# A two-layer attention and routed feed-forward block on one core: one VectorE subtraction a slot earlier, one group of weighted sums a step later

## The reference

```python
x = x + xattn(layernorm(x), ctx, ctx, w_q, w_k, w_v, w_o)      # 16 heads of 16, causal, softmax(q k / 4) v
q, k, v = (fff(layernorm(x), tree) for tree in "qkv")          # 4 routing levels, 16 leaves of 256 -> 64 -> 256
x = x + softmax(q k / 16) v
```

## Time and profile before

| What | Value |
|---|---|
| Median of 3 runs | 640.76 us (640.52 to 642.57) |
| Profiled execution, its own time | 640.1 us |
| Its span | 638.3 us |
| Mean granted TensorE clock | 0.965 |
| TensorE matmul busy | 586.1 us, 92% |
| VectorE busy | 439.1 us, 69% |
| ScalarE busy | 299.0 us, 47% |
| SyncE's DMA queue (q1) | 70.5% of 16 engines' time |

### The profile page before, as it was taken

One profiled execution on the slowest core, in us unless ns is written; L12 is line 12 of the kernel. 1 busy time (PEld: TensorE's weight loads), 2 busy tenths in 40 slices (PEclk: granted clock), 3 DMA queues, 4 the chain that ended last, 5 costly groups with the idle time before them and its releaser, 6 DMA issues.

```text
span 638.3 us, 14744 instructions
## 1 busy us (share of the span) xinstructions
PE 586.1 (92%) x5131; PEld 494.5 (77%) x5131; DVE 439.1 (69%) x1511; ACT 299.0 (47%) x482; POOL 236.9 (37%) x298
## 2 busy tenths in 40 slices
PE   8677999999899999999999897859999999799996
PEld 7566888877788887888888686848888888689995
DVE  2765666988788898898898787873555555156664
ACT  4104544544444453554445355007877787533331
POOL 6700010143143243334323326660006666666551
PEclk9869999999899999999999899879999999999999
DMA  6798788898998898899898749977999999766653
GB/s 190 221 305 261 237 230 226 252 260 238 283 271 249 286 310 247 258 297 283 251 296 275 208 134 303 309 254 274 324 364 387 411 408 375 258 191 197 200 177 126
DMA packets 99639, 169.58 MB, mean 266 GB/s; under 512 B 12848, under 2 KB 67824, under 8 KB 99568
## 3 DMA queue, kind: packets, MB, share of 16 engines
q1 hardware_dynamic: 87712, 141.83, 70.5%
q0 software_dynamic: 9216, 25.18, 12.5%
q10 hardware_dynamic: 2640, 1.65, 0.9%
HBM read 92.59 MB, written 75.50 MB: 263 GB/s over the span
## 4 chain that ended last, share of the span: by engine, by line
PE 51%; DMA 26%; SPq 13%; DVE 5%; issue 3%; ACT 1%; POOL 1%; DVEq 0%; ACTq 0%; POOLq 0%
DMA parts_dram<-k_lo 9%; DMA k<-parts_dram 8%; PE banks L840 6%; PE banks L825 6%; PE banks L814 6%; DMA parts_dram<-q_lo 5%; SPq L334 5%; PE banks L882 4%; PE banks L903 4%; PE banks L530 4%; PE banks L545 4%; PE banks L557 3%; SPq L317 2%; PE banks L871 2%; PE banks L573 2%
## 5 line engine op out<-in xcount | busy, mean ns | idle before, releaser
L1537 POOL DMA_INDIRECT xs_dram<-xn2s,place x96 | 95.7, 997 | 159.4 <-ACT pt L936 142.4
L1174 DVE TENSOR_REDUCE mneg<-banks 128x2 f32<-128x512 f32 x240 | 121.8, 548 | 44.9 <-PE banks L546 43.8
L936 ACT ACTIVATE pt<-banks 128x768 f32<-128x768 f32 x128 | 103.5, 810 | 102.2 <-PE banks L558 101.7
L545 PE MATMUL banks<-k,q 107*128 107x256 f32 x240 | 76.4, 369 | 17.7 <-DMA k<-parts_dram 10.9
L557 PE MATMUL banks<-q,k 109*128 109x256 f32 x256 | 74.0, 341 | 2.0 <-DMA q<-m_lo 0.3
L545 PEld LDWEIGHTS banks<-k,q 107*128 107x128 f32 x240 | 46.5, 194 | 29.3 <-DMA k<-parts_dram 16.3
L558 PE MATMUL banks<-q,k 109*128 109x128 f32 x256 | 57.3, 224 | 0.0
L573 PE MATMUL banks<-pt,vp 128*32 128x256 f32 (+1 forms) x1024 | 56.4, 339 | 0.4 <-ACT pt L936 0.4
L1596 POOL DMA_INDIRECT q_all<-ys_dram,place x32 | 30.8, 964 | 67.1 <-DMA ys_dram<-yb 53.8
L546 PE MATMUL banks<-k,q 107*128 107x128 f32 x240 | 54.4, 227 | 0.0
L557 PEld LDWEIGHTS banks<-q,k 109*128 109x128 f32 x256 | 48.7, 190 | 6.8 <-ACT pt L936 5.7
(11 more groups left out here) (177 smaller groups left out, 1290.9 us busy)
## 6 DMA issues: line engine op xcount, KB each, us to landing
ys_dram<-yb SPq DMA_DIRECT2D x36, 512.0 KB, 6.2
xb<-xs_dram SPq DMA_DIRECT2D x35, 512.0 KB, 7.7
k<-parts_dram SPq DMA_DIRECT2D x128, 128.0 KB, 3.8
q<-parts_dram SPq DMA_DIRECT2D x64, 256.0 KB, 4.6
xs_dram<-zero SPq DMA_DIRECT2D x45, 256.0 KB
xs_dram<-zero SPq DMA_DIRECT2D x18, 384.0 KB, 4.8
tables<-leafw SPq DMA_DIRECT2D x16, 257.0 KB, 8.2
xt<-x SPq DMA_DIRECT2D x16, 256.0 KB, 4.9
```

The source lines that it names most:

```text
L545: mm(ps[:, 0:S], q[0:KN, t, P:S], k[0:KN, t, :], start=True, stop=True)
L936: nc.scalar.activation(pt[:, 2 * p:2 * p + 2, :], st_banks(b, p)[:, :, 0:S + P], ACT.Exp, scale=SC).then_inc(exp_sb, 1)
L1174: last = nc.vector.tensor_reduce(mneg[1 - u][:, t, 2 * j:2 * j + 2], S_BANKS[:, :, cols], axis=AX.X, op=ALU.max, negate=True)
L1537: gp.indirect_dma_start(xs_dram[tree], bass.IndirectOffsetOnAxis(ap=place[:, k:k + 1], axis=0), xn2s[m % RING][:, t, :], None).then_inc(sc ...
```

## The change

On VectorE the subtraction for the low part of k of batch b + 2 moves from slot 4 (behind the maxima of that slot, ahead of `divide`) to slot 3, behind norm_in and ahead of part 4 of `allocate`. On TensorE, group 0 of the weighted sums of batches 0 to 14 moves from step b, slot 7, to step b + 1, slot 0, where it stands behind the transposes of the maxima and ahead of group 1. Group 1 thereby stands behind these transposes too; in step 15 it did before. The last batch keeps its group 0 at j = 6. No matmul, no transfer and no semaphore is added or removed.

```diff
-                    if j == 3 + lag(b) and has(b, 0):
+                    if j == 3 + lag(b) and b == NB - 1:
                         weigh(b, u, 0)
                     if j == 0 and b >= NB:
                         rank(b, u)
                         if b > NB:
                             warm(IDLE[2 if b == NB + 1 else 5])
-                    if j in (0, 2) and has(b, -1) and not (j == 0 and b == NB - 1):
-                        weigh(b - 1, 1 - u, j // 2 + 1)
                     if j == 0 and has(b, 0) and b < NB - 1:
                         maxima_T(b, u)
-                    if j == 0 and b == NB - 1:
-                        weigh(b - 1, 1 - u, 1)
+                    if j == 0 and has(b, -1):
+                        for r in ((0, 1) if b < NB else (1,)):
+                            weigh(b - 1, 1 - u, r)
+                    if j == 2 and has(b, -1):
+                        weigh(b - 1, 1 - u, 2)
...
                     if j == 3 and has(b, 3):
                         norm_in(b + 3, n + 1 + u, 1 - u)
+                    if j == 3 and has(b, 2):
+                        low_part(b, u, k_hi, k_lo, kh_sb, kl_sb)
                     if j == 3 and has(b, -3) and b < NB:
                         allocate(b - 3, 4)
...
-                    if j == 4 and has(b, 2):
-                        low_part(b, u, k_hi, k_lo, kh_sb, kl_sb)
                     if j == 4 and has(b, -1):
                         divide(b, 0)
```

## The result

| | Before | After |
|---|---|---|
| Median | 642.48 us (6 runs, 640.52 to 647.16) | 652.33 us (6 runs, 649.88 to 657.85) |
| Profiled execution: time, span | 640.1, 638.3 us | 651.27, 649.1 us |

The ratio is 1.0177, 95% interval 1.0139 to 1.0214: some 11.4 us (the two medians by themselves are 9.9 us apart, a ratio of 1.0153, inside the interval). The forecast was +6.6 us with a range that ended at +10.7. The direction was right and the size was not.

What follows compares the result with a forecast made beforehand. No one engine was taken as the bound: TensorE's order, the transfer chain and VectorE lay close together. Steps 6 to 12 +3.7, step 13 +0.7, steps 1 to 3 +2.7, step 14 -0.8, step 15 +0.3: +6.6, 647.4 us, range 642.0 to 651.5.

Steps and rivals of the forecast that it cites:

- nothing is saved where the group leaves: TensorE, slot 7: transposed scores 4 still wait for ScalarE's exponential; no gain, and a hole of about 1 us opens.
- +0.79 where it arrives: TensorE, slot 0 of the next step: group 0 adds its full 0.79 us, or 0 where transfers hold the step.
- VectorE's +0.59: Slots 4 and 5: k_lo delays the maxima and the next scores, 0 to 0.59 us a step, taken as 0.59.
- k_lo brings nothing: SyncE's unload of k: k_lo one slot earlier gains zero, since q_lo's transfer covers it by 1.2 us.
- a relief of 0.8 us in step 14: Step 14: added group halves a 1.53 us wait; half of the 1.7 us half-clock cost comes back, -0.8 us.
- rival F: Clock falls in each step's hole, 1.7 us each: 669 us if in all 13 steps, 652 in three; chance 0.08.
- steps 6 to 12: Attention pipeline: each step grows from 22.40 to TensorE's new work, 22.93 us; +3.7 us over seven steps.
- steps 1 to 3: Attention pipeline at lower DMA load: 3 x 0.79 + 0.3 = +2.7 us.
- steps 4 and 5: Attention pipeline: at 24.54 us each they exceed TensorE's new 22.93, so 0.
- step 13: Attention pipeline, 21.80 us before the change: +0.7 us.
- start of step 1, all behind step 13: Pipeline's end: step 14 adds 0 and gets 0.8 us of clock back, step 15 adds +0.3; the end -0.5 us.
- the queue of transfers catches up: Steps 4 to 12: a standing DMA queue absorbs the chain's later start; step is larger of old time and 22.93 us.

Runs made afterwards that it cites:

- the change's second measurement: The change itself measured again, on another chip, against the kernel before: ratio 1.0192 [1.0146, 1.0239].
- The hole alone: Kernel before, with group 0 of the weighted sums in slot 2 of the next step, k_lo still in slot 4: ratio 1.0186 [1.0132, 1.0240].
- with the projection in the hole: Kernel before, with group 0 in slot 2 of the next step and the output projection ahead of transposed scores 4: ratio 1.0031 [0.9997, 1.0065].
- The change with its hole filled: The change, with group 0 also computed at its old place, uncounted: ratio 1.0090 [1.0055, 1.0125] against the kernel before.
- The kernel with the projection in the hole: Kernel before, with group 0 in the next step's slot 0 and the output projection between transposed scores 3 and 4: ratio 1.0129 [1.0079, 1.0179].
- the chain started sooner: Kernel before, with the last transposed scores of a batch ahead of the scores in slot 2: ratio 0.9893 [0.9853, 0.9934].
- the second profile of the kernel before: Kernel before measured against itself, nothing changed: ratio 1.0017 [0.9976, 1.0058].

## Why the prediction was wrong in size

**Right: nothing is saved where the group leaves.** In slot 7 the wait of 0.90 us for ScalarE is there in each step, as forecast from the earlier trace rows. From the scores of j = 7 to those of the next step pass 4.67 us after the change, and 4.66 in the kernel with only k_lo moved, where the group is still there and no stack is waited for.

**Right: +0.79 where it arrives.** The scores of j = 1 start 279.00 - 276.28 = 2.72 us behind those of j = 0, against 201.14 - 199.14 = 2.00 before: +0.72 for a forecast of +0.79. The 32 matmuls of the two groups are seen as one row of 1.51 us above.

**Right: VectorE's +0.59.** VectorE in step 9, then TensorE's scores of j = 4 and j = 5:

```profile
263.85 0.25 DVE L1101 BATCH_NORM_AGGREGATE mv<-st 128x2 f32<-128x6 f32 x2 [0.17 <-DVE st L1096]
264.01 0.66 DVE L1127 TENSOR_TENSOR k_lo<-banks,k_hi 128x512 fp32r<-128x512 f32 x1
264.59 0.18 DVE L1279 TENSOR_SCALAR pages<-cnt_i 128x48 int32<-128x48 int32 x1
...
265.26 1.00 DVE L1175 TENSOR_REDUCE mneg<-banks 128x2 f32<-128x512 f32 x2
```
```profile
263.88 0.38 PE L545 MATMUL banks<-k,q 107*128 107x256 f32 x1
...
266.31 0.39 PE L545 MATMUL banks<-k,q 107*128 107x256 f32 x1 [0.40 <-DVE mneg L1175]
```

2.43 us lie between them, against 1.83 in step 6 before: +0.60. And k_lo brings nothing, as forecast from the earlier trace rows.

**Wrong: the clock as a rival and not as a term.** This is the step that failed. The sum counted the clock only as a relief of 0.8 us in step 14, and left the falls behind the new hole to rival F (669 in all 13 steps, 652 in three) with a chance of 0.08, on the ground that one wait of 1.11 us had no fall behind it. So the sum itself priced them at nothing. Its own price for three falls, 652, is where the time came out, but that is luck: there are three in steps 6 to 12 alone and more ahead of them, and other terms came out smaller than forecast. The runs show that the same hole of 0.90 us is followed by a fall in some steps and not in others, 1.7 us each. By stretches, profile against profile:

| Stretch | Forecast | Measured | Of it clock |
|---|---|---|---|
| steps 1 to 3 | +2.7 | 73.07 - 67.97 = +5.1 | 11.8 us at half clock for 3.4: (11.8 - 3.4) / 2 = +4.2 |
| steps 4 and 5 | 0 | 47.52 - 49.08 = -1.6 | about 0, one fall each |
| steps 6 to 12 | +3.7 | 165.94 - 156.82 = +9.1 | three falls, 3 x 1.68 = +5.0 |
| step 13 | +0.7 | 22.23 - 21.80 = +0.4 | 0 |
| start of step 1, all behind step 13 | -0.5 | +0.2 - 2.5 = -2.3 | less: 6.8 us at half clock behind step 13 for 20.5 |
| sum | +6.6 | +10.8 | about +9.2 ahead of step 14 |

Without the falls, steps 6 to 12 give +4.1 for a forecast of +3.7. Ahead of step 14 as a whole they leave 13.0 - 9.2 = +3.8 for a forecast of +7.1, so the other terms were too high: steps 1 to 5 give -0.7 for +2.7. For step 13 the sum had +0.7 without a working; its own rule gives 22.93 - 21.80 = +1.1. Three pairs of kernels that differ in whether the hole is filled price it in time: 1.0177 and 1.0090, 1.0155 and 1.0024, 1.0186 and 1.0031, that is 0.9 to 1.5%, 6 to 10 us. In a fourth, 1.0155 and 1.0129, the filling shortened TensorE's order until it waited for the stack, and nothing clear was gained.

The granted clock of all runs, not only of the profiled ones, says the same. Take (1 - mean granted clock) x span as an upper estimate of what the lower clock costs a run. On the chip of the change's second measurement it is 19.1 us for the kernel before and 25.7 for the change: +6.6 of the 11.9 us between their spans, which leaves 5.3 for everything else, where the forecast had +7.4 and a relief of 0.8 by the clock. In the change's first six runs it is 28.3; in the runs of the kernel before on four chips it is 19.1 to 20.9. The hole alone has 33.7, that is +14.6, and gains 4.4 elsewhere; with the projection in the hole it has 23.3. The change with its hole filled has 17.2, below the kernel before.

The rule named with rival F (the Trainium skill, "TensorE: Matmul & The Clock Gate", section "HAM oscillation — how this bites in real kernels": a wait repeated in each turn of a loop can drop the clock each turn) fits better than the forecast allowed. The page's example has waits for transfers several times as long, and a fall in every turn. The forecast had let it hold for long waits alone; here it holds for one of 0.90 us, in 6 of 12 turns.

**Wrong, without effect on the sum: the queue of transfers catches up.** The kernel with the projection in the hole shows that the chain keeps its length when it starts later, 16.8 us against 16.9. The forecast of 22.93 held because TensorE's order was the longer of two bounds that lie close together; in the change TensorE hardly waits for a stack. The DMA share of 1.05 in the earlier trace rows, from which the forecast took the catching up, had no say in that. Nor do the transfers set a fixed 22.4 us: the hole alone runs steps of 22.14 us without a wait for them.

**Open.** Which holes of one length are followed by a fall, and why the hole alone has more of them than the change, so that the two are the same within their intervals; by how much each of the remaining costs (slot 0, VectorE, transfers) adds to the time; and what the chain started sooner gains from.

## What to carry to other kernels

Work that stands inside a wait costs nothing there, and moved out it is paid in full; find its cover before moving it. A hole of a microsecond that recurs on TensorE in each turn of a loop should go into the sum as a share of turns with a clock fall, beside the idle time, and if the wait can't be removed, other work, even idle work, can be put into it, which paid in three pairs of four here. Where two bounds of a step lie within 2% of each other, making one shorter shows little; an experiment that shortens one well below the other tells which is which.

## What the runs showed of the hardware that was not expected

- A wait of 0.90 us of TensorE is followed by a stretch of 3.4 us at half the clock in some turns of a loop and not in others (in the first profile of the change behind 6 of the 12 holes that end between 80 and 345 us). A step with one is 1.68 to 1.71 us longer. Longer waits don't decide it either: in the second profile of the kernel before, waits for the stack of 1.67 and 1.54 us had a fall behind them and one of 1.58 us had none.
- In the kernel with the hole alone, the four stretches shown start 23.9 us apart from each other (151.8, 175.7, 199.6, 223.5), in steps of 23.83 to 23.85 us. Step 8 (226.98 to 249.12) is the first without one, at 22.14 us, and steps 9 to 12 have none either, at 22.15 to 22.16. With the one ahead of them, at 127.94, the five stretches start 0.66, 0.70, 0.76, 0.80 and 0.86 us behind the end of a hole; the next hole ends at 246.47 and has none behind it.
- The mean step differs between two profiles of one kernel by 22.85 - 22.40 = 0.45 us, some 0.2 of it by one clock fall, the rest by waits for transfers: more than many of the effects looked for.
